# A one-core vision network: ScalarE's copy of the turned gate values moved ahead of half of the normed tokens, and GpSimd's factors of the second norm made in one pass

## The reference, cut to what matters

```python
# h: (64, 6, 256), 384 tokens
h = h + L1_ffn(layernorm(h), gate_w, ln_gamma, ln_beta, fc1s, b1s, fc2s, b2s)

def L1_ffn(x, ...):
    xf = x.reshape(-1, d)                          # already normed once
    k = bs // n                                    # 48
    scores = (jnp.tanh(xf @ gate_w.T) + 1.0) * 0.5
    vals, idx = jax.lax.top_k(scores.T, k)         # per expert
    y = xf[flat_idx].reshape(k, n, d)
    y = _layernorm(y, ln_gamma, ln_beta)           # the second norm
    h = gelu(einsum('knd,nfd->knf', y, fc1s) + b1s)
    o = (einsum('knf,ndf->knd', h, fc2s) + b2s) * kept_w[:, :, None]
    return xf.at[flat_idx].add(o)
```

## Time and profile before

| | us |
|---|---|
| median of 3 runs | 232.57 |
| lowest and highest | 232.18, 232.72 |
| the profiled execution, whole | 233.47 |
| its span, first to last instruction | 231.7 |
| PE busy | 218.0 |
| VectorE busy | 131.9 |
| ScalarE busy | 73.8 |
| GpSimd busy | 56.3 |

### The profile page before, as it was taken

The page is one execution under the profiler, slowest core; times in us unless marked ns, Lnnn a source line. Parts: engine busy times, 40 slices in busy tenths (PEclk is TensorE's granted clock), DMA queues, the critical chain, the costliest instruction groups (busy, mean ns, idle before and its releaser), DMA issues.

```text
span 231.7 us, 3969 instructions
## 1 busy us (share of the span) xinstructions
PE 218.0 (94%) x1432; PEld 172.5 (74%) x1432; DVE 131.9 (57%) x419; ACT 73.8 (32%) x184; POOL 56.3 (24%) x122
## 2 busy tenths in 40 slices
PE   7999999999969999999999999999797899999995
PEld 5788888889958797778768867978676764655673
DVE  2597657576577475547865664864769525231212
ACT  2124242185676446013411621040036143130310
POOL 1043662266522123020232320300046150000000
PEclk9999999999999999859999997999999799999999
DMA  6999545940000000029999991000001204884002
GB/s 172 345 358 362 207 111 147 433 201 1 3 0 1 3 0 3 0 62 420 429 318 301 422 429 72 3 0 0 3 1 41 78 19 114 340 348 109 0 0 68
DMA packets 9747, 34.31 MB, mean 148 GB/s; under 512 B 1280, under 2 KB 3840, under 8 KB 7424
## 3 DMA queue, kind: packets, MB, share of 16 engines
q1 hardware_dynamic: 9728, 34.07, 40.9%
HBM read 32.88 MB, written 0.39 MB: 144 GB/s over the span
## 4 chain that ended last, share of the span: by engine, by line
PE 77%; DVE 9%; ACT 4%; issue 3%; POOL 3%; DMA 2%; SPq 2%; DVEq 0%; POOLq 0%; ACTq 0%
PE bank L451 16%; PE bank L1040 6%; PE bank L1014 6%; PE bank L676 5%; PE bank L685 5%; PE bank L575 4%; PE bank L600 3%; PE bank L553 3%; PE bank L743 2%; PE bank L440 2%; PE bank L982 2%; PE bank L755 2%; PE bank L463 2%; PE bank L1047 2%; DMA bench<-patches 2%
## 5 line engine op out<-in xcount | busy, mean ns | idle before, releaser
L451 PE MATMUL bank<-desk,bench 118*126 118x256 f32 x190 | 43.9, 381 | 0.2
L451 PEld LDWEIGHTS bank<-desk,bench 118*126 118x126 f32 x190 | 34.6, 188 | 6.2 <-DMA bench<-patches 0.9
L440 PE MATMUL bank<-zeros 128*128 128x256 f32 x94 | 28.2, 424 | 1.1 <-POOL small L1994 1.1
L1999 POOL TENSOR_TENSOR small<-small 96x2 f32<-96x2 f32 (+2 forms) x15 | 9.9, 659 | 70.5 <-DVE small L1312 51.3
L440 PEld LDWEIGHTS bank<-zeros 128*128 128x128 f32 x94 | 17.6, 206 | 3.9 <-POOL small L1994 1.1
L1747 ACT ACTIVATE attic<-bank,cols 128x126 f32<-128x126 f32 x38 | 15.2, 453 | 13.6 <-PE bank L463 13.4
L1094 DVE TENSOR_REDUCE bench<-bench 118x70 f32<-118x630 f32 x19 | 14.7, 798 | 6.5 <-DMA bench<-patches 6.4
L1740 ACT ACTIVATE desk<-bank 126x256 f32<-126x256 f32 x19 | 7.3, 384 | 25.7 <-PE bank L451 22.2
L2007 POOL TENSOR_TENSOR small<-small 126x1 f32<-126x1 f32 x19 | 10.5, 565 | 16.3 <-DVE small L1100 11.6
L685 PE MATMUL bank<-layw,bench 128*96 128x256 f32 x48 | 13.2, 424 | 1.4 <-DVE bench L1421 1.0
L676 PE MATMUL bank<-bench,layw 128*128 128x192 f32 x72 | 13.1, 331 | 0.5 <-ACT bench L1803 0.4
(11 more groups left out here) (220 smaller groups left out, 403.2 us busy)
## 6 DMA issues: line engine op xcount, KB each, us to landing
attic<-experts SPq DMA_DIRECT2D x10, 1024.0 KB, 8.1
desk<-experts SPq DMA_DIRECT2D x6, 1024.0 KB, 15.8
bench<-patches SPq DMA_DIRECT2D x19, 315.0 KB, 4.7
desk<-tokenizer_w SPq DMA_DIRECT2D x4, 576.0 KB, 5.9
layw<-layer_w SPq DMA_DIRECT2D x1, 2184.0 KB, 11.4
attic<-bias SPq DMA_DIRECT2D x8, 256.0 KB, 12.0
cons<-constants SPq DMA_DIRECT2D x1, 1258.0 KB, 5.5
desk<-conv_w SPq DMA_DIRECT2D x5, 128.0 KB, 3.6
```

The costliest lines, as they stand in the source:

```text
L440: mm(bank[b][:, 0:C], zeros[:, 0:P], zeros[:, :], start=True, stop=True)
L451: i = mm(conv_bank[t % 2][0:TP, 0:C], xt[t % XRING][0:KP, k, :], convw[0:KP, k, :], start=(k == 0), stop=(k == KX - 1))
L1999: pool.tensor_tensor(rs, var, half[0:parts, 0:rs.shape[1]], ALU.pow).then_inc(s(name), 1)
```

## The change

ScalarE's copy to `valT` is moved from behind both halves of `base` to between `xh2` of half 0 and `xh2` of half 1. On GpSimd the second calls of `rs_and_shift`, one for each half, become one function, `shift_both`, whose eight operations each cover both halves. ScalarE's wait in `norm_again` is for the same count (5) in both halves. The first calls of `rs_and_shift` do what they did. No arithmetic is changed.

```diff
             def norm_again(g):
 
-                act.wait_ge(s("again"), 5 * (g + 1))
+                act.wait_ge(s("again"), 5)
...
             norm_again(0)
+            act.wait_ge(s("vals_turned"), 1)
+            ac(valT, bank[5][:, 0:UT * E8].rearrange("p (t e) -> p t e", e=E8), ACT.Copy)\
+                .then_inc(s("valT_ready"), 1)
             norm_again(1)
             with_norm(1, 0)
             with_norm(1, 1)
-            act.wait_ge(s("vals_turned"), 1)
-            ac(valT, bank[5][:, 0:UT * E8].rearrange("p (t e) -> p t e", e=E8), ACT.Copy)\
-                .then_inc(s("valT_ready"), 1)
...
+            def shift_both():
+
+                mean, rs, nm = t_mv[0:TR, :, 0], t_rs[0:TR], t_nm[0:TR]
+                for g in range(G):
+                    pool.wait_ge(s(f"t_rs_ready{g}"), 4)
+                pool.tensor_tensor(t_sq[0:TR], rs, rs, ALU.mult).then_inc(s("again"), 1)
+                pool.wait_ge(s("again"), 1)
+                pool.tensor_scalar(t_again[0:TR], t_sq[0:TR], -EPS, 1.0 + EPS, ALU.mult, ALU.add)\
+                    .then_inc(s("again"), 1)
+                pool.wait_ge(s("again"), 2)
+                rsqrt(t_again[0:TR], t_sq[0:TR], "again", parts=TR)
+                pool.wait_ge(s("base_ready"), G)
+                pool.tensor_scalar(nm, mean, -1.0, None, ALU.mult).then_inc(s("nm_ready"), 1)
+                pool.wait_ge(s("again"), 3)
+                pool.tensor_tensor(t_s2[0:TR], rs, t_sq[0:TR], ALU.mult).then_inc(s("again"), 1)
+                pool.wait_ge(s("again"), 4)
+                pool.wait_ge(s("nm_ready"), G + 1)
+                pool.tensor_tensor(t_d2[0:TR], nm, t_s2[0:TR], ALU.mult).then_inc(s("again"), 1)
+                pool.tensor_scalar(t_up[0:TR], rs, 1.0, None, ALU.add).then_inc(s("up_ready"), G)
+                pool.tensor_tensor(t_dn[0:TR], nm, rs, ALU.mult).then_inc(s("shift_ready"), G)
...
-            rs_and_shift(3, 0, 1)
-            rs_and_shift(3, 1, 1)
+            shift_both()
             pool.memset(ysT, 0.0).then_inc(s("cleared"), 1)
```

More of the change, by code:

```diff
@@ L2077, in rs_tokens, with rs_and_shift @@
                 rsqrt(t_mv[0:TR, sl, 1], t_rs[0:TR, sl], f"t_rs_ready{g}", parts=TR)
-            def shift_again(g):
+            def rs_and_shift(g):
                 sl = slice(TG * g, TG * (g + 1))
[L2082 to L2100, removed]
+                rs_tokens(0, g)
                 pool.tensor_scalar(t_nm[0:TR, sl], t_mv[0:TR, sl, 0], -1.0, None, ALU.mult).then_inc(s("nm_ready"), 1)
[L2102 to L2105, removed]
+                pool.wait_ge(s(f"t_rs_ready{g}"), 1)
+                pool.wait_ge(s("nm_ready"), g + 1)
                 pool.tensor_scalar(t_up[0:TR, sl], t_rs[0:TR, sl], 1.0, None, ALU.add).then_inc(s("up_ready"), 1)
@@ L2192, in _ @@
             probs(9)
-            rs_and_shift(0, 0, 0)
+            rs_and_shift(0)
             rs_local(1)
@@ L2197, in _ @@
             clear_latents(0)
-            rs_and_shift(0, 1, 0)
+            rs_and_shift(1)
             rs_tokens(2, 0)
```

## The result

The changed kernel took 230.68 us (median of 4 runs: 228.43, 229.01, 232.35, 235.63), against 232.44 for the kernel before (4 runs, 232.18 to 232.72). The ratio given with it, 0.984 with a 95% interval of 0.981 to 0.987, rests on the runs least disturbed by the clock, 228.43 and 229.01 on the side of the changed kernel. The forecast was 231.8 us. So the direction was right, and the size was wrong: 1.8 us by the medians and 3.7 by that ratio, in place of 0.75.

What follows compares the result with a forecast made beforehand. PE's matmuls, busy 94% of the span, were taken as the bound, with valT alone holding the ranking before the gather. Median 232.57 - 0.75 (valT) + 0 (one pass) + 0 (transfers) = 231.82 us; range 230.6 to 232.7.

Steps and rivals of the forecast that it cites:

- 0.75: PE's transpose of line 964, before the gather: moving valT was to start it earlier, gaining 0.75 us.

Runs made afterwards that it cites:

- valT alone: Kernel before with only ScalarE's valT copy moved, GpSimd keeping its two passes: 228.33 us at a mean clock of 1.00, mean 231.83 us over 17 executions.

## What to carry to other kernels

Look at the mean granted clock of each execution before comparing two times: below a few per cent, compare executions at the full clock, or fit the time against the us at half clock over many executions and compare the lines. Compare spans as well as times. A wait with two sources is worth what the second source leaves: here both edits brought valT in front of the cut, which was ready 0.83 us before the old copy released PE (179.45 and 180.28 us), so one of them was enough. Where a kernel's gain is less than one stretch at half clock (1.15 us here), a median of four says little on it.

## What was not expected of the hardware

Warm-up matmuls can hold PE when the clock falls among them. In the second profile of the changed kernel it fell at 174.8 us, at the start of the nine:

```profile
174.62 5.84 PE L440 MATMUL bank<-zeros 128*128 128x256 f32 x18
180.39 0.22 PE L964 MATMUL bank<-cons,bench 8*128 8x8 f32 x1
```

They took 5.84 us instead of 4.15. VectorE's cut was ready at 179.25, the transpose came 1.1 us later without any idle time before it, and the gather began 10.46 us behind VectorE's first row (172.64), later than the 10.15 of the kernel before: in this execution the gain was gone.

One execution of the kernel before and one with valT alone took 313 and 314 us, at mean clocks of 0.646 and 0.644. The trace of the latter shows a third level between the two others; it is there from 5 us on, and in stretches of 0.5 us as well, so it is no mean of the two:

```profile
10.00:100.00 90.00, 88.14 (x395) 0.65 0.35 123
```

Nothing here tells where it came from. Both are left out of the means.
